# A graph network on one core: which engine subtracts the row maximum of a group's fourth graph

## The chip, the core and the metric

The kernel runs on one core of a Trainium2 chip. The core has five engines with a queue of instructions each: TensorE (PE in the profile; its weight loads stand apart as PEld), VectorE (DVE), ScalarE (ACT), GpSimd (POOL) and SyncE (SP), which here only issues DMAs. Engines wait for each other through semaphores. On-chip memory is SBUF, and PSUM for what TensorE writes. The metric is the device time of one execution in microseconds (us), the median of several runs; lower is better.

## What is computed

64 graphs of 128 nodes with 128 features go through four layers, each on the layer norm and ReLU of what came before and each added to its input: graph attention, a two-layer network on summed neighbours, a graph convolution, and five steps of a gated recurrent unit. The change lies in the softmax of the attention:

```python
def _L0_gnn_ref(x, adj, W, a):
    h = jnp.einsum('bni,io->bno', x, W).reshape(x.shape[0], x.shape[1], H, D)   # H = 4, D = 32
    ...
    e = e_i[:, :, :, None] + e_j[:, :, None, :]
    e = jnp.where(e > 0, e, LRELU_SLOPE * e)
    e = jnp.where(adj[:, None, :, :] > 0, e, NEG_INF)
    attn = jax.nn.softmax(e, axis=-1)
    out = jnp.einsum('bhnm,bhmd->bhnd', attn, h)
    ...
...
h = jnp.maximum(_layernorm(x, axis=-1), 0.0)
x = x + _L0_gnn_ref(h, adj, L0_gnn_W, L0_gnn_a)
h = jnp.maximum(_layernorm(x, axis=-1), 0.0)
x = x + _L1_gnn_ref(h, adj, L1_gnn_eps, L1_gnn_W1, L1_gnn_b1, L1_gnn_W2, L1_gnn_b2)
h = jnp.maximum(_layernorm(x, axis=-1), 0.0)
x = x + _L2_gnn_ref(h, adj, L2_gnn_weight, L2_gnn_bias)
h = jnp.maximum(_layernorm(x, axis=-1), 0.0)
x = x + _L3_gnn_ref(h, adj, nodemask, L3_gnn_weight, L3_gnn_w_ih, L3_gnn_w_hh, L3_gnn_b_ih, L3_gnn_b_hh)
```

## The kernel before

Nodes lie on the 128 partitions, and x stays in SBUF. The graphs are taken in 16 **groups** of four. A first stage (`first_layers`, some 265 us) computes the first three layers, a second one (`gru_layer`) the recurrent layer, with four groups in flight, and it is almost all matmuls.

The first stage is a software pipeline. It has one **slot** a group, and in a slot each engine works on up to eight groups at different depths: `at(n)` is the group that entered n slots ago. The order of each engine's work in a slot is written out by hand in its own `slot(at, number)`; nothing is scheduled or planned. A wait stands in the queue of its engine, and what is behind it waits too.

The attention's scores of a group are made for `at(2)`. TensorE writes the four heads of graph g, with the mask, to PSUM bank g. Then, for g = 0 to 3:

- ScalarE's `leaky` (L1092) takes a leaky ReLU from PSUM to the SBUF tile `prob` (128 x 4 heads x 128), after `score_ready`;
- VectorE's `row_max` (L1259) writes the maximum of each row and head to `row_max` (128 x 4), and raises `max_done`;
- GpSimd's `less_max` (L712) waits for that and subtracts the maximum from `prob` in place, and raises `shifted`;
- ScalarE's `exponential` (L1097) waits for `shifted`; TensorE's `turn_prob` (L862) transposes the heads to PSUM; `keep_probT` copies them back to SBUF, graphs 0 and 2 on ScalarE (L1102), graphs 1 and 3 on VectorE (L1263), graphs 2 and 3 in the next slot.

In the next slot TensorE's `attend` multiplies by the projected nodes, its first half after graphs 0 and 1 and its second after graphs 2 and 3, and `sum_up` takes the softmax's sums. VectorE copies both out (L1267, L1271), takes the reciprocal of the sums when TensorE has transposed them (L891, L1276), multiplies (L1281) and adds to x (L1286). TensorE's last masks of the following group, `mask(at(2), 2)` and `mask(at(2), 3)`, wait for these, since they write the same banks, and its scores stand behind them.

VectorE's slot goes on behind the fourth maximum with `add_out(at(4), 0)` (L1292, x plus the second layer), the `moments` of two layer norms (L1223, L1229), `keep_probT(at(2), 1)` and `add_out(at(5), 1)`. The next slot begins with `shift_of` (L1234), a tiny instruction (128 x 4) that reads `mean_var` and `rstd` in SBUF, for which ScalarE's `normalise` (L1061) waits, and `keep_probT(at(3), 3)`. In slot 4 the largest gate weight is found (`all_rows_max`, L272) just behind the fourth maximum, and TensorE's `turn_max` (L276) waits for it.

GpSimd's slot: `add_self` (L699, adds the self loops to the transposed adjacency), `centre` for layer norm 3 (L721), `bias` (L706), `scale` (L728), `bias`, `scale`, the four `less_max`, and `centre` for layer norm 0, which waits until TensorE has transposed the y of the group before. All are 128 x 512 in SBUF.

Of the kernel before, what the change touches and what calls it, by code (L numbers as in the profile page):

```python
# [24 lines left out]
GRAPHS, NODES, DIM = 64, 128, 128  # L25
HEADS = 4
# [4 lines left out]
GROUP = 4  # L31
# [496 lines left out]
def first_layers(nc, io, t, psum, tiles, gru, score_weights, recurrent, ctx):  # L528

    def sem(name):  # L530
        return ctx.enter_context(nc.semaphore(name))
# [5 lines left out]
    gone, prob, probT, top, attT = tiles.gone, tiles.prob, tiles.probT, tiles.top, tiles.attT  # L537
# [27 lines left out]
    lrelu_done = sem("lrelu_done")  # L565
    max_done = sem("max_done")
    shifted = sem("shifted")
    exp_done = sem("exp_done")
    probT_psum = sem("probT_psum")
    probT_act = sem("probT_act")  # L570
# [121 lines left out]
    def gpsimd(pool):  # L692
        wait_apart = apart(pool, "gpsimd")

        def add_self(group):
            pool.wait_ge(adjT_ready, group.count)
            if group.before(2).exists:
                pool.wait_ge(z_psum[0], group.before(2).count)
            pool.tensor_tensor(adjT1[group.odd][:, :, :], adjT[group.odd][:, :, :],  # L699
                               t["self_eye"][:, :].unsqueeze(1).to_broadcast([128, GROUP, 128]), ALU.add)\  # L700
                .then_inc(adjT1_ready, 1)

        def bias(group, n, b):

            wait_apart(y_ready[n + 1], group.count)
            pool.tensor_tensor(xs(group), xs(group), b[:, :].unsqueeze(1).to_broadcast([128, GROUP, DIM]), ALU.add)\  # L706
                .then_inc(biased[n], 1)

        def less_max(group, g):

            pool.wait_ge(max_done, group.graph_count(g))
            pool.tensor_tensor(prob[:, g, :, :], prob[:, g, :, :],  # L712
                               top[:, g, :].unsqueeze(2).to_broadcast([128, HEADS, NODES]),
                               ALU.subtract).then_inc(shifted, 1)

        def centre(group, n):

            wait_apart(var_ready[n], group.count)
            if group.before(1).exists:
                wait_apart(yT_psum if n == 0 else h0T_psum, group.before(1).count)  # L720
            pool.tensor_tensor(y[n][:, :, :], xs(group), mean_var[n][:, :, 0:1].to_broadcast([128, GROUP, DIM]),  # L721
                               ALU.subtract).then_inc(centred[n], 1)

        def scale(group, n):

            pool.wait_ge(rstd_ready[n], group.count)
            pool.wait_ge(centred[n], group.count)
            pool.tensor_tensor(y[n][:, :, :], y[n][:, :, :],  # L728
                               rstd[n][:, :].unsqueeze(2).to_broadcast([128, GROUP, DIM]), ALU.mult)\
                .then_inc(y_ready[n], 1)  # L730
# [9 lines left out]
        def slot(at, number):  # L740
            if at(4):
                add_self(at(4))
            if at(6):
                centre(at(6), 3)
            if number == 4:
                pool.wait_ge(gru.layers_loaded, gru.all_layers_loaded)
            if at(4):
                bias(at(4), 0, t["b2"])
            if at(6):
                scale(at(6), 3)  # L750
            if at(5):
                bias(at(5), 1, t["b3"])
            if at(1):
                scale(at(1), 0)
            if at(2):
                less_max(at(2), 0)
                less_max(at(2), 1)
                less_max(at(2), 2)
                less_max(at(2), 3)
            if at(0):  # L760
                centre(at(0), 0)

# [282 lines left out]
    def scalar(act):  # L1045
# [47 lines left out]
                .then_inc(lrelu_done, 1)  # L1093

        def exponential(group, g):
            act.wait_ge(shifted, group.graph_count(g))
            a.activation(prob[:, g, :, :], prob[:, g, :, :], ACT.Exp, scale=t["gates_b"][:, E_UNSCALE:E_UNSCALE + 1])\  # L1097
                .then_inc(exp_done, 1)

# [12 lines left out]
        def slot(at, number):  # L1112
# [48 lines left out]
            if at(2):  # L1161
                exponential(at(2), 0)
# [53 lines left out]
    def vector(dve):  # L1216
        v = nc.vector
        wait_apart = apart(dve, "vector")

        def moments(group, n, signal, count):  # L1220
            wait_apart(signal, count)
            for g in range(GROUP):
                last = v.bn_stats(stats[n][:, g, :], t["x"][:, group.graph(g), :])  # L1223
            last.then_inc(stats_done[n], 1)
            wait_apart(stats_done[n], group.count)
            if n in (0, 3) and group.before(1).exists:
                wait_apart(y_ready[n], group.before(1).count)
            for g in range(GROUP):
                last = v.bn_aggr(mean_var[n][:, g, :], stats[n][:, g, :])  # L1229
            last.then_inc(var_ready[n], 1)  # L1230

        def shift_of(group, n):
            dve.wait_ge(rstd_ready[n], group.count)
            v.scalar_tensor_tensor(shift[n][:, :], mean_var[n][:, :, 0], -1.0, rstd[n][:, :], ALU.mult, ALU.mult)\  # L1234
                .then_inc(shift_ready[n], 1)
# [21 lines left out]
        def row_max(group, g):  # L1257
            dve.wait_ge(lrelu_done, group.graph_count(g))
            v.tensor_reduce(top[:, g, :], prob[:, g, :, :], AXIS.X, ALU.max).then_inc(max_done, 1)  # L1259

        def keep_probT(group, g):
            dve.wait_ge(probT_psum, group.graph_count(g))
            v.tensor_copy(probT[:, g, :, :].rearrange("p h n -> p (h n)"), P[:, g, :]).then_inc(probT_dve, 1)  # L1263

        def keep_attended(group):
            dve.wait_ge(att_psum, group.count)
            v.tensor_copy(flat(attT[:, :, :]), P[:, 0, :]).then_inc(att_kept, 1)  # L1267
# [27 lines left out]
        def slot(at, number):  # L1295
            if number == 5:
                gru.whole_max(dve)
            if number == 7:
                gru.max_bits(dve)
            if number == 0:  # L1300
                score_weights.sum_rows(dve)
            if at(4):
                shift_of(at(4), 1)
            if at(3):
                keep_probT(at(3), 3)
            if at(6):
                moments(at(6), 3, x_added[1], at(6).count)
            if number == 18:
                gru.split_hi(dve)
            if at(2):  # L1310
                find_gone(at(2))
            if at(3):
                keep_attended(at(3))
                keep_sums(at(3))
            if at(5):
                shift_of(at(5), 2)
            if at(2):
                keep_e_lo(at(2))
            if at(3):
                divide(at(3))  # L1320
                add_attended(at(3))
            if at(2):
                find_edges(at(2))
            if number == 2:
                score_weights.self_weight(dve)
            if at(3):
                moments(at(3), 1, x_attended, at(3).count)
            if number == 3:
                gru.row_max(dve, 0, 2)
            if number == 18:  # L1330
                recurrent.parts(dve, 0)
            if at(2):
                row_max(at(2), 0)
            if number == 6:
                gru.biases(dve)
            if at(2):
                row_max(at(2), 1)
            if number == 7:
                gru.exponent(dve)
            if at(2):  # L1340
                row_max(at(2), 2)
            if number == 7:
                gru.scale_bits(dve)
            if at(2):
                row_max(at(2), 3)
            if number == 4:
                gru.row_max(dve, 2, 4)
                gru.row_max(dve, 4, 6)
                gru.all_rows_max(dve)
            if at(4):  # L1350
                add_out(at(4), 0, B_TURN)
            if number == 7:
                gru.scales(dve)
            if at(0):
                moments(at(0), 0, x_loaded[at(0).odd], at(0).loads)
            if number == 0:
                score_weights.row_max(dve)
            if number == 1:
                score_weights.whole_max(dve)
                score_weights.scale(dve)  # L1360
            if at(4):
                moments(at(4), 2, x_added[0], at(4).count)
            if number == 7:
                gru.scaled_biases(dve)
            if number == 18:
                gru.split_lo(dve, GRU_STEPS, GRU_STEPS + 1)
            if at(2):
                keep_probT(at(2), 1)
            if at(5):
                add_out(at(5), 1, B_EDGE)  # L1370
# [378 lines left out]
```

## Time and profile before

| | us |
|---|---|
| median of 3 runs | 652.4 (651.42 to 653.29) |
| the profiled execution | 651.48 |
| its span, from first to last instruction | 649.3 |
| TensorE, VectorE, ScalarE, GpSimd busy | 609.8, 574.0, 520.2, 402.8 |

The profile is one execution. Busy shares are taken over both stages. A row of the timeline is: start, length, engine, line, operation, output<-inputs, partitions x elements and type, xN for N alike in a row and, in brackets, the idle time of the engine before it and what ended it. Instructions of one engine overlap a little at their ends. Of line numbers, those of `kernel.py` before the change are meant.

### The profile page before, as it was taken

To read this page: it belongs to the slowest core of one execution; us is meant where nothing else is said; L and a number is where in the kernel's file an instruction comes from. 1 tells how busy PE (TensorE), PEld (TensorE's weight loads), DVE (VectorE), ACT (ScalarE), POOL (GpSimd) and SP (SyncE) were. 2 spreads that over 40 slices of the span, in tenths; PEclk is the share of its full clock that TensorE was granted. 3 is DMA by queue.
4 is the path that set the end of the run, shared out by engine and by line. 5 is a ranking of instruction groups with operands and counts; after the bars stand their busy time and mean duration, and the time that the engine had idled before them with its cause. 6 is when DMAs were issued, how large, how long until landed. Compare 5 with 4: busy or idle time off the path is not lost. (4 is left out here: it accounts for less than half of the span.)

```text
span 649.3 us, 14511 instructions
## 1 busy us (share of the span) xinstructions
PE 609.8 (94%) x5068; PEld 391.4 (60%) x5068; DVE 574.0 (88%) x1384; ACT 520.2 (80%) x964; POOL 402.8 (62%) x363
## 2 busy tenths in 40 slices
PE   2877999999999999799999999999999999999995
PEld 1566887878888888555544455555455555555552
DVE  3478988888998888878898999999999999999995
ACT  2566998999999999667877887877877877877874
POOL 3354677778888776745766655655655655555554
PEclk9888999999999999999999999999999999999998
DMA  7201010101010000112232333433333433333432
GB/s 152 66 18 49 19 49 19 49 19 50 19 51 28 24 18 3 34 36 48 58 57 49 66 64 67 82 78 70 65 63 69 82 82 66 66 81 68 82 80 67
DMA packets 114696, 35.91 MB, mean 55 GB/s; under 512 B 87680, under 2 KB 114624, under 8 KB 114624
## 3 DMA queue, kind: packets, MB, share of 16 engines
q1 hardware_dynamic: 113424, 34.79, 25.2%
q8 instruction: 41, 0.67, 0.4%
q10 hardware_dynamic: 1200, 0.20, 0.2%
q14 instruction: 31, 0.25, 0.1%
HBM read 9.80 MB, written 4.19 MB: 22 GB/s over the span
## 5 line engine op out<-in xcount | busy, mean ns | idle before, releaser
L1650 POOL TENSOR_TENSOR h0T<-r,zh 128x512 f32<-128x512 f32 x80 | 101.6, 1270 | 142.6 <-DVE r L1687 142.3
L52 PE MATMUL psum<-h_parts,gru_w 128*128 128x512 f16 x720 | 183.0, 380 | 2.9 <-DVE r L1691 2.8
L52 PE MATMUL psum<-t_parts,gru_w 128*128 128x512 f16 x720 | 181.5, 379 | 0.0
L52 PEld LDWEIGHTS psum<-h_parts,gru_w 128*128 128x128 f16 x720 | 69.9, 98 | 85.6 <-DVE r L1691 16.1
L1644 POOL TENSOR_TENSOR zh<-z,h0T 128x512 f32<-128x512 f32 x80 | 101.8, 1273 | 11.2 <-ACT z L1622 11.2
L52 PEld LDWEIGHTS psum<-t_parts,gru_w 128*128 128x128 f16 x720 | 66.8, 98 | 66.4 <-DVE t_parts L1674 6.9
L1619 ACT CAST t_parts<-psum 128x512 f16<-128x512 f32 x80 | 46.9, 586 | 62.2 <-PE psum L52 62.1
L1532 DVE CAST h_parts<-h0T 128x512 f16<-128x512 f32 x80 | 79.9, 999 | 3.0 <-POOL h0T L1650 3.0
L1627 ACT ACTIVATE r<-r,gates_b 128x512 f32<-128x512 f32 x80 | 65.0, 812 | 9.5 <-DVE r L1678 6.7
L712 POOL TENSOR_TENSOR prob<-prob,row_max 128x512 f32<-128x512 f32 x64 | 64.5, 1040 | 12.2 <-DVE row_max L1259 11.6
L1622 ACT ACTIVATE z<-psum,gates_b 128x512 f32<-128x512 f32 x80 | 62.3, 778 | 5.8 <-PE psum L52 0.9
L721 POOL TENSOR_TENSOR y<-x_all,mean_var 128x512 f32<-128x512 f32 x32 | 34.4, 1074 | 49.0 <-DVE mean_var L1229 23.7
L1632 ACT ACTIVATE r<-psum,gates_b 128x512 f32<-128x512 f32 x80 | 61.1, 763 | 3.3 <-PE psum L52 3.3
L1691 DVE SCALAR_TENSOR_TENSOR r<-psum,gates_b,r 128x512 f32<-128x512 f32 x80 | 59.6, 744 | 2.3 <-ACT r L1632 2.3
L1624 ACT ACTIVATE zc<-psum,gates_b 128x512 f32<-128x512 f32 x80 | 61.6, 769 | 0.0
L1674 DVE TENSOR_TENSOR t_parts<-psum,t_parts 128x512 f16<-128x512 f32 x80 | 54.6, 682 | 6.2 <-ACT t_parts L1619 6.2
L1687 DVE TENSOR_TENSOR r<-r,zc 128x512 f32<-128x512 f32 x80 | 56.4, 705 | 2.7 <-ACT r L1627 2.7
L1223 DVE BATCH_NORM_STATS2 stats<-x_all 128x6 f32<-128x128 f32 x256 | 54.9, 277 | 4.0 <-DMA x_all<-in_x 3.2
L1534 DVE TENSOR_TENSOR h_parts<-h0T,h_parts 128x512 f16<-128x512 f32 x80 | 55.4, 692 | 2.7
L1061 ACT ACTIVATE y<-x_all,shift,rstd 128x128 f32<-128x128 f32 x128 | 52.7, 488 | 2.5 <-DVE shift L1234 2.4
L1678 DVE TENSOR_TENSOR r<-psum,r 128x512 f32<-128x512 f32 x80 | 54.4, 680 | 0.0
L52 PEld LDWEIGHTS psum<-edges,h_nodes 128*128 128x128 f16 x640 | 42.4, 98 | 18.7 <-issue 0.3
(145 smaller groups left out, 1123.8 us busy)
## 6 DMA issues: line engine op xcount, KB each, us to landing
x_all<-in_x SPq DMA_DIRECT2D x16, 256.0 KB, 4.0
adj<-in_adj SPq DMA_DIRECT2D x16, 256.0 KB, 3.0
out_x<-y SPq DMA_DIRECT2D x14, 256.0 KB, 2.5
h_nodes<-h_parts SPq DMA_TRANSPOSE x80, 3.1
out_x<-zT SPq DMA_DIRECT2D x2, 256.0 KB, 2.3
gw<-in_L_gnn_weight SPq DMA_DIRECT2D x1, 320.0 KB, 5.7
W<-in_L_gnn_W SPq DMA_DIRECT2D x2, 128.0 KB, 2.7
wi<-in_L_gnn_w_ih SPq DMA_DIRECT2D x1, 192.0 KB, 7.1
```

The source lines that it names most:

```text
L52: return nc.tensor.matmul(out, lhsT, rhs, start=start, stop=stop)
L712: pool.tensor_tensor(prob[:, g, :, :], prob[:, g, :, :], top[:, g, :].unsqueeze(2).to_broadcast([128, HEADS, NODES]), ALU.subtract).then_i ...
L1532: v.tensor_copy(by_graph(hp[now.s][:, 0, :]), state(now)).then_inc(hi_ready, 1)
L1534: v.tensor_tensor(by_graph(hp[now.s][:, 1, :]), state(now), by_graph(hp[now.s][:, 0, :]), ALU.subtract)\
L1622: a.activation(z[one.s][:, :], one.Z, ACT.Sigmoid, bias=col(B_Z), scale=col(UNSCALE))\
L1624: a.activation(zc[one.s][:, :], one.Z, ACT.Sigmoid, bias=col(B_NZ), scale=col(N_UNSCALE))\
L1627: a.activation(r[one.s][:, :], r[one.s][:, :], ACT.Tanh, bias=col(B_IN), scale=col(UNSCALE))\
L1632: a.activation(r[here.s][:, :], here.R, ACT.Sigmoid, bias=col(B_R), scale=col(UNSCALE))\
L1644: pool.tensor_tensor(by_graph(zh[now.s][:, :]), by_graph(z[now.s][:, :]), state(now), ALU.mult)\
L1650: pool.tensor_tensor(state(now), by_graph(r[now.s][:, :]), by_graph(zh[now.s][:, :]), ALU.add)\
L1687: v.tensor_tensor(r[two.s][:, :], r[two.s][:, :], zc[two.s][:, :], ALU.mult).then_inc(mixed, 1)
L1691: v.scalar_tensor_tensor(r[one.s][:, :], one.N, col(B_HN), r[one.s][:, :], ALU.add, ALU.mult)\
```

## The change

GpSimd's slot has three `less_max` instead of four. VectorE gets `less_last`, the same subtraction for g = 3, right behind its fourth `row_max`; it waits for that maximum and raises a new semaphore, `last_shifted`. ScalarE's exponential of g = 3 waits for the new semaphore, and those of g = 0 to 2 count three a group.

```diff
@@ -756,7 +757,6 @@
                 less_max(at(2), 0)
                 less_max(at(2), 1)
                 less_max(at(2), 2)
-                less_max(at(2), 3)
             if at(0):
                 centre(at(0), 0)
 
@@ -1093,7 +1093,10 @@
         def exponential(group, g):
-            act.wait_ge(shifted, group.graph_count(g))
+            if g == GROUP - 1:
+                act.wait_ge(last_shifted, group.count)
+            else:
+                act.wait_ge(shifted, group.number * (GROUP - 1) + g + 1)
             a.activation(prob[:, g, :, :], prob[:, g, :, :], ACT.Exp, scale=t["gates_b"][:, E_UNSCALE:E_UNSCALE + 1])\
                 .then_inc(exp_done, 1)
@@ -1258,6 +1261,14 @@
+        def less_last(group):
+
+            g = GROUP - 1
+            dve.wait_ge(max_done, group.graph_count(g))
+            v.tensor_tensor(prob[:, g, :, :], prob[:, g, :, :],
+                            top[:, g, :].unsqueeze(2).to_broadcast([128, HEADS, NODES]),
+                            ALU.subtract).then_inc(last_shifted, 1)
+
@@ -1343,6 +1354,7 @@
             if at(2):
                 row_max(at(2), 3)
+                less_last(at(2))
```

VectorE's queue from the row maxima of a group in the middle of the first stage to the copy of the fourth transposed graph, before:

```order
L1259 TENSOR_REDUCE row_max<-prob 128x4 x4
L1292 TENSOR_TENSOR x_all<-psum,x_all 128x512
L1223 BN_STATS stats<-x_all 128x6 x4
L1229 BN_AGGR mean_var<-stats 128x2 x4
L1223 BN_STATS stats<-x_all 128x6 x4
L1229 BN_AGGR mean_var<-stats 128x2 x4
L1263 COPY probT<-psum 128x512
L1292 TENSOR_TENSOR x_all<-psum,x_all 128x512
L1234 SCALAR_TENSOR_TENSOR shift<-mean_var,rstd 128x4
L1263 COPY probT<-psum 128x512
```

The same with the change (its lines have moved by 3 to 11):

```order
L1262 TENSOR_REDUCE row_max<-prob 128x4 x4
L1268 TENSOR_TENSOR prob<-prob,row_max 128x512
L1303 TENSOR_TENSOR x_all<-psum,x_all 128x512
L1226 BN_STATS stats<-x_all 128x6 x4
L1232 BN_AGGR mean_var<-stats 128x2 x4
L1226 BN_STATS stats<-x_all 128x6 x4
L1232 BN_AGGR mean_var<-stats 128x2 x4
L1274 COPY probT<-psum 128x512
L1303 TENSOR_TENSOR x_all<-psum,x_all 128x512
L1237 SCALAR_TENSOR_TENSOR shift<-mean_var,rstd 128x4
L1274 COPY probT<-psum 128x512
```

One instruction stands between the maxima and the sum that was next; what follows keeps its order.

GpSimd's queue at the same place, from the subtractions to the bias of the next slot, before:

```order
L712 TENSOR_TENSOR prob<-prob,row_max 128x512 x4
L721 TENSOR_TENSOR y<-x_all,mean_var 128x512
L699 TENSOR_TENSOR adjT<-adjT,self_eye 128x512
L721 TENSOR_TENSOR y<-x_all,mean_var 128x512
L706 TENSOR_TENSOR x_all<-x_all,b 128x512
```

With the change:

```order
L713 TENSOR_TENSOR prob<-prob,row_max 128x512 x3
L722 TENSOR_TENSOR y<-x_all,mean_var 128x512
L700 TENSOR_TENSOR adjT<-adjT,self_eye 128x512
L722 TENSOR_TENSOR y<-x_all,mean_var 128x512
L707 TENSOR_TENSOR x_all<-x_all,b 128x512
```

The fourth subtraction is gone, and nothing else has moved.

## Rows read from the trace of the kernel before

**Rows 1.** The page: busy us and share; a group: xcount | busy, mean ns.

```profile
PE 609.8 (94%) x5068; PEld 391.4 (60%) x5068; DVE 574.0 (88%) x1384; ACT 520.2 (80%) x964; POOL 402.8 (62%) x363
...
L712 POOL TENSOR_TENSOR prob<-prob,row_max 128x512 f32<-128x512 f32 x64 | 64.5, 1040 | 12.2 <-DVE row_max L1259 11.6
```

**Rows 2.** Windows: stretch, length, busy of PE PEld DVE ACT POOL, PEclk, DMA.

```profile
36.51:52.71 16.20, 13.36 (x148) 10.30 (x148) 11.22 (x35) 12.07 (x26) 8.63 (x8) 0.89 0.07 18
...
100.64:117.38 16.74, 15.21 (x183) 12.38 (x183) 14.44 (x59) 14.79 (x38) 11.86 (x12) 1.00 0.06 17
117.38:132.06 14.68, 14.68 (x182) 12.31 (x182) 13.10 (x52) 14.55 (x36) 11.86 (x12) 1.00 0.19 55
...
161.43:176.36 14.93, 14.89 (x182) 12.28 (x182) 13.38 (x52) 14.68 (x37) 11.86 (x12) 1.00 0.07 20
...
220.55:235.24 14.69, 14.69 (x182) 12.31 (x182) 13.10 (x52) 14.56 (x36) 11.73 (x12) 1.00 0.07 21
```

**Rows 3.** Timeline of ScalarE in the interval from 146.75: exponentials 2 and 3, normalising.

```profile
151.88 1.34 ACT L1097 ACTIVATE prob<-prob,gates_b 128x512 f32<-128x512 f32 x2
...
154.60 1.66 ACT L1061 ACTIVATE y<-x_all,shift,rstd 128x128 f32<-128x128 f32 x4
```

**Rows 4.** Timeline of VectorE in the same interval.

```profile
147.38 2.46 DVE L1259 TENSOR_REDUCE row_max<-prob 128x4 f32<-128x512 f32 x4 [0.40 <-ACT prob L1092]
149.76 0.68 DVE L1292 TENSOR_TENSOR x_all<-psum,x_all 128x512 f32<-128x512 f32 x1
...
154.23 0.15 DVE L1234 SCALAR_TENSOR_TENSOR shift<-mean_var,rstd 128x4 f32<-128x4 f32 x1
154.30 0.68 DVE L1263 COPY probT<-psum 128x512 f32<-128x512 f32 x1
...
158.31 0.26 DVE L1276 RECIPROCAL rsum<-psum 128x16 f32<-128x16 f32 x1 [0.32 <-PE psum L891]
...
159.34 0.69 DVE L1286 TENSOR_TENSOR x_all<-psum,x_all 128x512 f32<-128x512 f32 x1
```

**Rows 5.** Timeline of TensorE in the same interval: attention's second half, last masks.

```profile
155.15 0.62 PE L52 MATMUL psum<-probT,hW 128*32 128x128 f32 x16
...
160.26 0.59 PE L52 MATMUL psum<-gone,identb 128*128 128x512 bf16 x2
```

**Rows 6.** Timeline of GpSimd in the same interval: subtractions, self loops.

```profile
148.14 4.04 POOL L712 TENSOR_TENSOR prob<-prob,row_max 128x512 f32<-128x512 f32 x4
...
154.31 1.29 POOL L699 TENSOR_TENSOR adjT<-adjT,self_eye 128x512 f32<-128x512 f32 x1
```

**Rows 7.** L1687's durations (ns min/median/max); timelines of VectorE and GpSimd at 315.

```profile
L1687 DVE TENSOR_TENSOR r<-r,zc x80: 681/684/1532, 283.9 to 642.4; 128x512 f32<-128x512 f32 x80
...
315.31 1.53 DVE L1687 TENSOR_TENSOR r<-r,zc 128x512 f32<-128x512 f32 x1
...
315.18 1.11 POOL L721 TENSOR_TENSOR y<-x_all,mean_var 128x512 f32<-128x512 f32 x1
316.44 1.30 POOL L728 TENSOR_TENSOR y<-y,rstd 128x512 f32<-128x512 f32 x1
```

**Rows 8.** Timelines of VectorE and of GpSimd, interval from 161.43.

```profile
168.91 0.44 DVE L1234 SCALAR_TENSOR_TENSOR shift<-mean_var,rstd 128x4 f32<-128x4 f32 x1
...
168.28 1.04 POOL L721 TENSOR_TENSOR y<-x_all,mean_var 128x512 f32<-128x512 f32 x1 [1.42 <-PE psum L803]
169.28 1.28 POOL L699 TENSOR_TENSOR adjT<-adjT,self_eye 128x512 f32<-128x512 f32 x1
```

**Rows 9.** Timelines of VectorE and of GpSimd, interval from 100.64.

```profile
108.60 0.91 DVE L1234 SCALAR_TENSOR_TENSOR shift<-mean_var,rstd 128x4 f32<-128x4 f32 x1
...
108.20 1.29 POOL L699 TENSOR_TENSOR adjT<-adjT,self_eye 128x512 f32<-128x512 f32 x1
```

**Rows 10.** Timeline of TensorE, interval from 52.71.

```profile
57.87 0.27 PE L276 MATMUL psum<-ident,top 128*1 128x128 f32 x1 [3.20 <-DVE top L272]
```

**Rows 11.** Timeline of VectorE, interval from 235.24.

```profile
241.22 0.69 DVE L1263 COPY probT<-psum 128x512 f32<-128x512 f32 x1 [0.75 <-PE psum L862]
```

More of the change, by code:

```diff
@@ L567, in first_layers @@
     shifted = sem("shifted")
+    last_shifted = sem("last_shifted")
     exp_done = sem("exp_done")
```

## The prediction

> I call the stretch from the first leaky ReLU of one group (L1092 on ScalarE) to that of the next an **interval**. There are sixteen such starts, at 20.61 to 249.93 us, and the change acts once behind each.
>
> **What bounds the kernel now.** First the page's busy shares: TensorE 94%, VectorE 88%, ScalarE 80%, GpSimd 62% [rows 1]. They mix two stages. Everything touched here runs in the first 265 us; the recurrent stage behind is a row of matmuls that starts when the first stage lets it. So I split the first stage into its intervals [rows 2]. Eight in a row, from 117.38 to 235.24, are nearly alike: six last 14.68 or 14.69, one 14.83, one 14.93, with VectorE busy 13.10 of 14.68, ScalarE 14.55 and GpSimd 11.86. By busy time ScalarE is the bound and VectorE seems to have 1.6 to spare. The timeline says otherwise. In the interval from 146.75, VectorE ends the shift at 154.23 + 0.15 = 154.38 and the copy of the fourth transposed graph at 154.30 + 0.68 = 154.98 [rows 4]. ScalarE begins normalising, which needs that shift, at 154.60 [rows 3], and TensorE begins the second half of the attention, which needs that copy, at 155.15 [rows 5]. At the far end VectorE's residual sum ends at 159.34 + 0.69 = 160.03 [rows 4] and TensorE's last masks, which need it, start at 160.26; they stand just ahead of the scores for which the next leaky ReLU waits [rows 5]. So a second chain runs VectorE, TensorE, VectorE, TensorE, ScalarE and closes in the same 14.68. Between the row maxima and that copy VectorE has no wait for another engine in it.
>
> The interval from 161.43 shows how little slack that chain has. There the shift took 0.44 where it takes 0.15, 0.29 more [rows 8], and the interval lasted 14.93 where 14.68 is usual, 0.25 more [rows 2]. So a delay ahead of that copy goes into the interval but for 0.04.
>
> **Why that shift was long.** It reads two tensors in SBUF. In the same moment GpSimd ran its centring, 168.28 to 169.32; the shift ended at 169.35, 0.03 behind it, although GpSimd's next instruction had been taken up at 169.28 [rows 8]. In the interval from 100.64 the shift started at 108.60, inside GpSimd's self-loop addition of 108.20 to 109.49, took 0.91 and ended at 109.51 [rows 9]. A full tile does the same: the product at 315.31 took 1.53 where the median of its 80 is 0.684, and ended at 316.84, 0.55 behind GpSimd's instruction (315.18 + 1.11 = 316.29); GpSimd's next one, taken up meanwhile, ended at 317.74, 0.90 behind VectorE's [rows 7]. So a VectorE instruction with two SBUF inputs is held until the running GpSimd instruction ends, and then goes first. The Trainium skill, SBUF — State Buffer, section Who interferes with whom, has this rule: a VectorE instruction with two SBUF inputs and a GpSimd instruction that reads SBUF exclude each other for a whole instruction, the first to issue going first; the trace agrees. With it the interval costs what follows; without it, it would cost the first rival's price.
>
> **The change, part by part, in the interval from 146.75.**
>
> Taken away: the fourth of GpSimd's subtractions, which start 1.00 apart and take 1.04 each, 4.04 for four [rows 1, 6]. Who waits for it? The fourth exponential is the second of the pair at 151.88 to 153.22, and starts some 0.6 in, behind the third; the subtraction ended at 152.18 [rows 3, 6]. Next on GpSimd is a centring that waits for TensorE's transposes, which follow the second exponential, so it does not start earlier. I cost this edit at nothing: ScalarE's third exponential hides it.
>
> Added: on VectorE the same subtraction, with both inputs in SBUF (prob and row_max). The four maxima end at 147.38 + 2.46 = 149.84 [rows 4]. It can't read before GpSimd's second subtraction ends, at 148.14 + 1.00 + 1.04 = 150.18 [rows 6]; whatever its wait for its own maximum takes, up to 0.34, vanishes in that. By the product's row it ends 0.55 later, at 150.73. Not held, it would take 0.684. The residual sum behind it began 0.08 ahead of the maxima's end, at 149.76 [rows 4]; now it begins at 150.65, **0.89 later**. Queued behind it are eight statistics with their means, the copy of the second transposed graph, a residual sum, the shift and the copy of the fourth, all 0.89 late.
>
> Moved by that: GpSimd's third subtraction, held in its turn, ends at 150.73 + 0.90 = 151.63 where it ended at 151.18. The third exponential began at 151.88 [rows 3], so 0.25 is still spare. No cost, but thin cover.
>
> Moved too, and this decides: the shift goes from 154.23 to 155.12. Until now it fell just ahead of the self-loop addition, which starts at 154.31 and ends at 154.31 + 1.29 = 155.60 [rows 6]. That addition follows the centring, which follows TensorE and ScalarE, so it stays. The shift now falls inside it and ends 0.02 behind it, at 155.62, **1.24 later** than 154.38 [rows 4, 6, 9]. That holds for any delay from 0.1 to 1.1, so the price of the subtraction hardly matters. Less the 0.04 of slack: **+1.20 an interval**, 15.88. ScalarE waits about 1.1 for the shift, TensorE 1.2 for the copy. The second half of the interval hangs on these and moves as a whole; VectorE's wait of 0.32 for the transposed sums [rows 4] stays, since that work itself waits for VectorE.
>
> **The other intervals.** The two from 70.86 and 85.50 have the same order: +1.20 each. In the one from 100.64 the shift was already held to the end of the addition at 109.49 [rows 9]; 0.7 to 0.89 later it starts at 109.3 to 109.5 and ends about where it did: 0, at most 0.13. In the one from 52.71 TensorE waited 3.20 for VectorE's largest gate weight (L272), which stands behind the fourth maximum [rows 10]: +0.9, or 0.7 if nothing holds it. In the two from 235.24 and 249.93 VectorE waits 0.75 for a transposed graph behind that point [rows 11], which takes up nearly all of 0.89, and the addition comes earlier there: 0, at most 0.1 each. The first two are full of waits for TensorE: 0, give or take 0.3. The recurrent stage follows in program order and moves as a whole: 0.
>
> **Sum.** 0.9 + 2 x 1.20 + 8 x 1.20 = 12.9. The profiled execution took 651.48 (span 649.3); that gives 664.4. It lay 0.9 under the median of the three runs, 652.4, so for a median I say **665.3**.
>
> **Rivals.**
>
> Nothing is held at the shift. If the addition comes a little later, or such a small instruction slips in, an interval pays only the subtraction, 0.72 to 0.89 less 0.04: ten times 0.68 to 0.85 and 0.7 to 0.9 once, 7.5 to 9.4, so 660 to 662. Against it: both held shifts [rows 8, 9].
>
> GpSimd goes first. If its third subtraction gets the inputs ahead of VectorE's, VectorE starts after 151.18 and ends at 151.73: 1.89 late, 1.85 in ten intervals, about 1 in the one from 100.64, 1.9 in the one from 52.71 and 0.9 in each of the last two: 23, so 675. Against it: at 169.28 the waiting VectorE went first [rows 8]. For it: two full tiles contending have no row here.
>
> TensorE's clock. It idles 1.2 more in 15.9. The interval from 36.51 shows a mean granted clock of 0.89; in the one from 100.64, with 15.21 busy of 16.74, it stayed at 1.00 [rows 2], the 2.4 GHz level. New intervals would have 14.68 of 15.88, 92%, against 91% there, so I expect no fall. If it came, a clock of 0.89 would cost up to 0.11 x 15.9 = 1.7 in each of eight: 14 more, 679.
>
> It is hidden (not slower). If the bound were ScalarE's row of work alone, VectorE's waits of 0.40 ahead of the maxima and 0.32 ahead of the reciprocal [rows 4] would take the 0.72, and the time stays 652, 651.7 if the rare waits on the fourth subtraction go. It decides at the shift: it needs the shift's end to move by less than about 0.1. The Trainium skill, GPSIMD Engine Reference, section Key points, calls VectorE structurally about 2x faster at elementwise work; the rows show 1.04 against 0.684, and that speaks for the swap only where GpSimd's end is waited for. Against this rival: the interval from 161.43.
>
> **Chances.** Forecast 0.67, not held at the shift 0.14, GpSimd first 0.08, clock 0.05, hidden 0.06. The forecast's own range is 663 to 668, by the small terms left at nothing. The range of 8 in 10 takes in the first rival and an early share of the others: 659.5 to 671. Of the hidden case I give 0.02 to faster by over 0.3% (about what a measurement here can tell from no change) and 0.04 to within it; slower has 0.94.
>
> **What would show it.** In the new profile: eight intervals of about 15.9; VectorE's subtraction about 0.85 long; GpSimd's third one about 1.5; the shift about 0.5 long and ending with the self-loop addition; ScalarE's normalising waiting about 1.1 for it; granted clock 1.00; the recurrent stage as long as before. Intervals of 15.4 to 15.5 speak for the first rival, of 16.5 for GpSimd first, of 14.7 for the hidden one. Wrong would be, above all, my claim that the self-loop addition stays where it is while VectorE moves.

## The result and the profile after

The kernel with the change took 663.92 us (663.5 to 664.22, 4 runs) against 651.91 for the one before (650.79 to 653.29, 4 runs), a ratio of 1.0188 with a 95% interval of 1.0161 to 1.0215: **12.0 us slower**, where 12.9 and a time of 665.3 had been forecast. The profiled execution took 663.5, with a span of 661.4.

The windows of the kernel after, from one group's first leaky ReLU to the next one's (columns as in [rows 2]: busy PE, PEld, DVE, ACT, POOL, then the granted clock):

```profile
52.38:72.38 20.00, 15.64 (x163) 12.84 (x163) 16.05 (x49) 13.34 (x31) 7.97 (x7) 0.83 0.15 41
...
104.59:121.32 16.73, 15.44 (x183) 12.40 (x183) 14.29 (x60) 14.78 (x37) 11.32 (x11) 1.00 0.06 17
...
137.20:153.07 15.87, 15.16 (x182) 12.27 (x182) 14.29 (x53) 14.67 (x36) 11.29 (x11) 1.00 0.07 19
153.07:169.16 16.09, 15.38 (x182) 12.35 (x182) 14.41 (x53) 14.71 (x36) 11.51 (x11) 1.00 0.17 50
...
232.65:248.52 15.87, 15.17 (x182) 12.27 (x182) 14.28 (x53) 14.68 (x37) 11.29 (x11) 1.00 0.07 19
248.52:263.20 14.68, 14.68 (x182) 12.30 (x182) 12.92 (x45) 14.29 (x34) 10.69 (x10) 1.00 0.07 20
```

Against [rows 2]: the eight alike intervals have gone from 14.68 to 15.87, one of them to 16.09 (there VectorE's means have a gap of 0.21 that no wait explains); the one that held 16.74 still has 16.73; the last but one is 14.68 as before. The one from 52.38 has grown by 1.85, from the 18.15 between 52.71 and 70.86 in before, more than any.

VectorE's timeline in the interval from 137.20, which answers to [rows 4]:

```profile
140.33 0.85 DVE L1268 TENSOR_TENSOR prob<-prob,row_max 128x512 f32<-128x512 f32 x1
141.10 0.68 DVE L1303 TENSOR_TENSOR x_all<-psum,x_all 128x512 f32<-128x512 f32 x1
...
144.97 0.68 DVE L1303 TENSOR_TENSOR x_all<-psum,x_all 128x512 f32<-128x512 f32 x1
145.57 0.49 DVE L1237 SCALAR_TENSOR_TENSOR shift<-mean_var,rstd 128x4 f32<-128x4 f32 x1
145.98 0.68 DVE L1274 COPY probT<-psum 128x512 f32<-128x512 f32 x1
```

The source row of the new subtraction (durations in ns, min/median/max):

```profile
L1268 DVE TENSOR_TENSOR prob<-prob,row_max x16: 695/851/853, 23.7 to 266.3; 128x512 f32<-128x512 f32 x16
```

GpSimd's, which answers to [rows 6], and ScalarE's, which answers to [rows 3]:

```profile
138.59 3.48 POOL L713 TENSOR_TENSOR prob<-prob,row_max 128x512 f32<-128x512 f32 x3
143.76 1.04 POOL L722 TENSOR_TENSOR y<-x_all,mean_var 128x512 f32<-128x512 f32 x1 [1.69 <-PE psum L803]
144.76 1.28 POOL L700 TENSOR_TENSOR adjT<-adjT,self_eye 128x512 f32<-128x512 f32 x1
...
142.33 1.34 ACT L1100 ACTIVATE prob<-prob,gates_b 128x512 f32<-128x512 f32 x2
...
146.18 1.26 ACT L1061 ACTIVATE y<-x_all,shift,rstd 128x128 f32<-128x128 f32 x3 [1.00 <-DVE shift L1237]
```

The subtraction takes 0.85, and 0.695 at the least. GpSimd's three take 3.48, where three at 1.00 apart would take 3.04: its third one is 0.44 longer. The shift starts at 145.57, inside the self-loop addition of 144.76 to 146.04, and ends at 146.06. The residual sum just ahead of it runs inside the same addition and takes its usual 0.68: one of its two inputs is in PSUM. ScalarE, which had no wait ahead of its normalising [rows 3], waits 1.00 for the shift. The third exponential begins at 142.33, 5.13 into the interval, as before: what GpSimd's third subtraction lost stayed under cover.

### The profile page after: what moved, and what is told of

Same layout as the page of the kernel before. It is cut to its first block and busy times, and to the rows that moved or that the text cites. A ratio compares the mean times of both kernels' runs of the same rounds, so it can differ in the third digit from the quotient of the medians.

```text
span 661.4 us, 14511 instructions
## 1 busy us (share of the span) xinstructions
PE 613.2 (93%) x5068; PEld 391.0 (59%) x5068; DVE 589.5 (89%) x1400; ACT 521.1 (79%) x964; POOL 393.8 (60%) x347
## 5 line engine op out<-in xcount | busy, mean ns | idle before, releaser
L713 POOL TENSOR_TENSOR prob<-prob,row_max 128x512 f32<-128x512 f32 x48 | 55.8, 1189 | 11.9 <-DVE row_max L1262 11.3
```

The lines of the kernel that those rows point to most:

```text
L713: pool.tensor_tensor(prob[:, g, :, :], prob[:, g, :, :], top[:, g, :].unsqueeze(2).to_broadcast([128, HEADS, NODES]), ALU.subtract).then_i ...
```

## Experiments

Each run is compared with the kernel before on the same chip in the same batch, since the median of before went from 649.94 to 651.91 over the batches: after lay 12.0 above before in its own. The edits of the first six runs are made to the kernel after, those of the last section to the kernel before; `...` in a diff stands for lines left out.

### Nobody subtracts the fourth maximum

```diff
                 row_max(at(2), 3)
-                less_last(at(2))
...
-                act.wait_ge(last_shifted, group.count)
+                act.wait_ge(max_done, group.graph_count(g))
```

> The kernel after without VectorE's subtraction: the fourth graph's maximum is not subtracted at all, GpSimd subtracts three, and the fourth exponential waits for the fourth maximum. Theory (GpSimd's fourth subtraction cost nothing, VectorE's is the whole loss): intervals of 14.68 and the time of before, 651.9 within 0.7. Rival (GpSimd's fourth was on a path too, and the change gave part of its loss back): 1 to 3 us under before.

Measured: 650.91 against 650.26, a ratio of 1.0011 (0.9989 to 1.0034). All intervals from 73 us on are those of before to 0.01, but for the one of 14.93 there, which is 14.69 here:

```profile
134.51:149.19 14.68, 14.68 (x182) 12.30 (x182) 13.10 (x52) 14.55 (x37) 10.87 (x11) 1.00 0.07 21
```

GpSimd is busy 10.87 instead of 11.86 and nobody notices. Its fourth subtraction cost nothing, so taking it away could give nothing back, and the loss is all VectorE's. (The profiled execution, 654.19, was the longest of the ten; its first three intervals took 52.3 us where those of before took 50.3, with TensorE longer at its lower clock.)

### The self-loop addition moved ahead of the centring

```diff
         def slot(at, number):
-            if at(4):
-                add_self(at(4))
...
+            if at(3) and number != LAST + 3:
+                add_self(at(3))
             if at(0):
                 centre(at(0), 0)
```

> The kernel after, with GpSimd's self-loop addition moved from the head of a slot to the end of the slot before, behind the three subtractions, where GpSimd waits for TensorE. Theory (the shift is held by that addition): VectorE's shift starts 8.4 us into an interval as before and takes 0.15 instead of 0.50, the copy behind it starts 0.34 earlier, ten intervals of 15.87 become 15.53, and the time falls by 3.4, to 660.5. Rival (the interval pays only VectorE's new subtraction and nothing is held at the shift): intervals stay 15.87, the time 663.9.

Measured: 659.5 against 650.26, 1.0152 (1.0122 to 1.0181): 9.2 above before, where after was 12.0 above. Windows, VectorE and GpSimd of this run:

```profile
135.02:150.56 15.54, 15.17 (x182) 12.28 (x182) 13.96 (x53) 14.68 (x37) 11.32 (x11) 1.00 0.06 18
...
143.39 0.15 DVE L1237 SCALAR_TENSOR_TENSOR shift<-mean_var,rstd 128x4 f32<-128x4 f32 x1
143.46 0.68 DVE L1274 COPY probT<-psum 128x512 f32<-128x512 f32 x1
...
139.86 1.28 POOL L700 TENSOR_TENSOR adjT<-adjT,self_eye 128x512 f32<-128x512 f32 x1
141.58 1.04 POOL L722 TENSOR_TENSOR y<-x_all,mean_var 128x512 f32<-128x512 f32 x1 [0.44 <-PE psum L803]
```

The shift starts 8.37 into its interval, as in after, but now GpSimd has nothing running there, and it takes 0.15. Intervals are 15.53, to the hundredth that was forecast. So 0.34 of the 1.19 was the hold at the shift. No instruction of VectorE was touched. The time is less clear than the intervals: the span is 2.8 under after's, not 3.4. The intervals are together 4.7 shorter, 1.2 of it in the one from 52.76, where TensorE's clock was low for less long, and the recurrent stage is 1.7 longer, with a low stretch that after lacks (both below).

### One head instead of four

```diff
-            v.tensor_tensor(prob[:, g, :, :], prob[:, g, :, :],
-                            top[:, g, :].unsqueeze(2).to_broadcast([128, HEADS, NODES]),
+            v.tensor_tensor(prob[:, g, 0:1, :], prob[:, g, 0:1, :],
+                            top[:, g, 0:1].unsqueeze(2).to_broadcast([128, 1, NODES]),
                             ALU.subtract).then_inc(last_shifted, 1)
```

> The kernel after, with VectorE's subtraction cut to one of four heads (128 x 128 instead of 128 x 512); for the fourth graph the other three heads' maxima are not subtracted. Theory: the subtraction ends some 0.4 earlier, the shift starts at 7.97 instead of 8.37 us of an interval, is still inside the self-loop addition and ends with it, so the intervals stay 15.87 and the time stays 663.9 within 0.5. Rival (the price goes with the subtraction's length): intervals of 15.5, 4 us less, 659.9.

Measured: 663.51 against 650.26, 1.0213 (1.0186 to 1.0239), within 0.5 of after's 663.92, as forecast (13.3 above its own before, with the intervals of after). The subtraction's source row, the window, VectorE's shift and GpSimd's addition:

```profile
L1268 DVE TENSOR_TENSOR prob<-prob,row_max x16: 291/452/455, 23.9 to 266.2; 128x128 f32<-128x128 f32 x16
...
137.02:152.90 15.88, 14.94 (x182) 12.25 (x182) 14.30 (x53) 14.68 (x36) 10.91 (x11) 1.00 0.06 18
...
145.00 0.89 DVE L1237 SCALAR_TENSOR_TENSOR shift<-mean_var,rstd 128x4 f32<-128x4 f32 x1
...
144.59 1.28 POOL L700 TENSOR_TENSOR adjT<-adjT,self_eye 128x512 f32<-128x512 f32 x1
```

VectorE does 0.40 less in each interval and the interval is as long as ever. The shift comes 0.40 earlier and takes 0.40 longer, 0.89, until the addition ends at 145.87. By the busy share VectorE is as full as in after (14.30 of 15.88 against 14.29 of 15.87): the hold counts as busy.

### Both edits

> Both edits of the two runs before it: one head on VectorE (three heads' maxima of the fourth graph not subtracted) and the self-loop addition ahead of the centring. Theory: now the subtraction's length counts, since nothing holds the shift: it ends at about 8.12 us of an interval, intervals of 15.13, time 656.5. Rival: the same as with one head alone.

Measured: 656.6 against 650.26, 1.0101 (1.0073 to 1.0129).

```profile
133.88:149.02 15.14, 14.94 (x182) 12.25 (x182) 13.56 (x53) 14.67 (x36) 10.91 (x11) 1.00 0.07 20
...
141.85 0.15 DVE L1237 SCALAR_TENSOR_TENSOR shift<-mean_var,rstd 128x4 f32<-128x4 f32 x1
```

Now the 0.40 counts in full: 15.53 less 0.40 is 15.13. The four runs make a square of interval lengths:

| | addition behind the centring | addition ahead of it |
|---|---|---|
| four heads on VectorE | 15.87 | 15.53 |
| one head | 15.88 | 15.13 |

The subtraction's length has no effect in one column and its whole effect in the other. No price put on the subtraction alone can give that; a hold that ends with a GpSimd instruction does.

### The shift moved to another place

VectorE's queue alone is changed: both sets of statistics ahead of both sets of means, the shift between the means of the slot before, the residual sum ahead of the second copy.

```diff
-            if at(4):
-                shift_of(at(4), 1)
...
+            both = at(0) and at(4)
+            if both:
+                stats_of(at(0), 0, x_loaded[at(0).odd], at(0).loads)
+                stats_of(at(4), 2, x_added[0], at(4).count)
+                means_of(at(0), 0)
+                shift_of(at(3), 1)
+                means_of(at(4), 2)
```

> The kernel after, with VectorE's queue changed: both sets of statistics stand ahead of both sets of means (which saves the two waits of 0.26 and 0.15 for its own results), the shift of the second layer norm stands between the means, one slot earlier than its place ahead of the fourth copy, and the residual sum ahead of the copy of the second transposed graph. Theory (the shift's place among GpSimd's instructions made the difference between 0.85 and 1.20): the shift starts near 6.4 us of an interval, just ahead of GpSimd's centring at 6.56, is held by nothing, and the copy of the fourth graph starts at 8.04: intervals of 15.13, time 656.6 by the clock of the run after (8 to 9 us under it is too much, 7 is right). Rival (a hold always costs the same, wherever the shift stands): only the 0.4 of waits goes, intervals of 15.47.

Measured: 654.6 against 649.94, 1.0073 (1.0052 to 1.0094), 7.3 less above before than after was. The edit moves the residual sum, which the diff does not show. Window, the subtraction, the shift and the two copies behind it:

```profile
133.64:148.63 14.99, 14.76 (x182) 12.34 (x182) 13.76 (x53) 14.55 (x37) 11.30 (x11) 1.00 0.07 19
...
136.76 0.85 DVE L1274 TENSOR_TENSOR prob<-prob,row_max 128x512 f32<-128x512 f32 x1
...
139.96 0.14 DVE L1243 SCALAR_TENSOR_TENSOR shift<-mean_var,rstd 128x4 f32<-128x4 f32 x1
...
140.87 1.29 DVE L1280 COPY probT<-psum 128x512 f32<-128x512 f32 x2
```

The shift is not held, ScalarE does not wait for it, and the second copy of the pair starts at 7.82 of the interval, not 8.04: the reordering saved 0.2 more than I had counted. The interval follows: 7.82 is 0.27 later than before's 7.55, and 14.99 is 0.31 longer than 14.68, where 15.13 had been forecast. So three quarters of the loss can be had back while VectorE still does the subtraction; how much of them is the hold and how much the two waits saved, this run alone does not tell.

### The largest gate weight first

```diff
                 row_max(at(2), 3)
-                less_last(at(2))
             if number == 4:
                 gru.row_max(dve, 2, 4)
                 gru.row_max(dve, 4, 6)
                 gru.all_rows_max(dve)
+            if at(2):
+                less_last(at(2))
```

> The kernel after, with VectorE's new subtraction moved, in the fourth slot alone, behind the search for the largest gate weight. The interval from 52.4 grew from 18.14 to 20.00, where 0.9 had been forecast. Theory (0.7 of it is the subtraction ahead of that search, 1.2 is TensorE at its lower clock level for 6.8 us there instead of 3.4): TensorE waits 3.2 for the weight instead of 4.08, and the interval is 18.1 with one low stretch of 3.4, 19.3 with one of 6.8. Rival (the whole 1.9 is the subtraction): 18.1 either way.

One run: 664.06; no verdict on the time is possible from it. The interval came to 18.11 with one low stretch of the clock, which both theories gave. What tells them apart is the same interval in the other runs. After and the self-loops run both had the subtraction ahead of the search, and TensorE waited equally long for the weight, 4.08 and 4.09; but after had the lower clock level for 6.8 us, the self-loops run for 3.4. The wait of after, a window around its low stretch, the low stretch of the self-loops run, and then the interval in that run and in this one:

```profile
58.42 0.37 PE L276 MATMUL psum<-ident,top 128*1 128x128 f32 x1 [4.08 <-DVE top L272]
...
57.40:64.30 6.90, 5.88 (x27) 5.58 (x28) 4.67 (x22) 3.01 (x6) 0.00 (x0) 0.51 0.40 113
...
58.50:61.90 3.40, 3.10 (x14) 2.80 (x15) 3.00 (x18) 1.84 (x4) 1.18 (x1) 0.50 0.15 43
52.76:71.58 18.82, 14.35 (x163) 11.49 (x163) 15.82 (x49) 13.36 (x32) 8.00 (x7) 0.91 0.15 44
...
53.14:71.25 18.11, 14.53 (x163) 11.67 (x163) 16.02 (x49) 13.35 (x32) 7.53 (x7) 0.91 0.16 45
```

With a mean granted clock of 0.91 the interval is 18.11 with the subtraction behind the search and 18.82 with it ahead: 0.7 is its price. With a mean of 0.83 it is 20.00 in after: 1.2 more, which goes with TensorE at 1.2 GHz for 6.8 us instead of 3.4. The place of the self-loop addition makes no difference there: with one head the interval is 19.65 with the addition behind the centring and 19.69 with it ahead, both with 6.8 us of the lower level. Why the level stayed down twice as long is not shown, and the length of the wait does not tell: 4.09 went with 3.4 in the self-loops run and with 6.8 in the run with the shift moved. In before, which waited 3.20 until 57.87, the stretch began at 58.5, behind the wait; in after it began at 57.4, inside the wait. The recurrent stage of this run had a low stretch, 399.84 against after's 398.20, which takes back most of what the interval gained.

### Is there room in the kernel before?

The same three edits of VectorE's queue, made to the kernel before:

> The kernel before with the same three edits of VectorE's queue, and no subtraction on it. Theory (in before two chains tie at 14.68, VectorE's and ScalarE's row of work): VectorE's copy can start 0.26 earlier, but ScalarE is full, so intervals stay 14.68 and the time stays that of before within 0.7. Rival (VectorE's chain alone sets the interval): intervals of 14.42, 2.6 to 3.4 less.

> The kernel before with VectorE's queue changed, a second time and in more rounds. Intervals of 14.68 as in the first; it lay 0.25% under before, which is the two stray delays of 0.25 and 0.15 in the profile of before and the clock in the recurrent stage. Theory: 0.1 to 0.4% under before. Rival: no difference.

Measured: 649.27 against 649.94, 0.9975 (0.9953 to 0.9997), and again 649.69 against 650.16, 0.998 (0.9961 to 0.9998). The intervals from 117 us on are 14.68, all of them: VectorE's copy comes earlier (7.29 into the interval for 7.55) and the interval is no shorter, as it must if another row of work is full. What has changed is the intervals that were longer in before:

```profile
101.53:117.14 15.61, 14.96 (x183) 12.45 (x183) 13.50 (x59) 14.66 (x38) 11.87 (x12) 1.00 0.07 18
```

That is the interval of 16.74 in [rows 2], whose shift took 0.91 [rows 9]: 1.1 shorter, of which 0.76 is the length of the hold; the rest fits the waits that the new order saves, and the two were not separated. The one of 14.93, whose shift was held too, is at 14.68, and so is the one of 14.83, whose shift had taken 0.15: there VectorE's means had a gap of 0.17 that no wait explains. Together that is 1.5, of which the time shows some 0.5 to 0.7; in both profiles of this version TensorE's clock was low for longer in the first three intervals, which came to 52.1 instead of 50.3, and not low at all at the start of the recurrent stage (below). So a gain is shown in the intervals, most of it from the moved shift; how much of the 0.2% is it and how much the clock is not.

Then, with VectorE's queue as in the last run, ScalarE was relieved too, and the self-loop addition put behind the subtractions:

```diff
+        def root_0(group):
+            pool.tensor_tensor(log_var[0][:, :], mean_var[0][:, :, 1], eps_tile[:, :], ALU.add)\
+                .then_inc(eps_added[0], 1)
+            pool.wait_ge(eps_added[0], group.number - 1)
+            pool.tensor_tensor(rstd[0][:, :], log_var[0][:, :], half_tile[:, :], ALU.pow).then_inc(rstd_ready[0], 1)
...
-            if at(1):
+            if at(1) and number < 3:
                 rstd_of(at(1), 0)
```

> The run before it (before with VectorE's queue changed) with ScalarE relieved as well: from the third group on, the inverse deviation of the first layer norm (two ScalarE instructions, 0.48 a slot) is computed by GpSimd behind its centring, with the power that it uses for the last groups, and the self-loop addition stands behind the subtractions. Theory (both chains shorter): ScalarE's row needs 14.20, VectorE's copy of the fourth graph can't start before TensorE's transposes end, at 7.29 instead of 7.55 of an interval, so intervals of about 14.42, and 2.5 to 3.5 less than before. Rival (ScalarE alone sets the interval): 14.20, 5 less.

Measured: 652.26 against 649.94, 1.0034 (1.0011 to 1.0058), with intervals of 15.22. I had walked into the thing under study. The shift had been moved to 5.43 of the interval and the self-loop addition, by the other edit, to the same moment:

```profile
139.37 1.25 DVE L1249 SCALAR_TENSOR_TENSOR shift<-mean_var,rstd 128x4 f32<-128x4 f32 x1
...
139.32 1.28 POOL L699 TENSOR_TENSOR adjT<-adjT,self_eye 128x512 f32<-128x512 f32 x1
```

So the addition was made to wait for the shift:

```diff
         def add_self(group):
             pool.wait_ge(adjT_ready, group.count)
+            pool.wait_ge(shift_ready[1], group.count)
```

> The run with both chains relieved again, but GpSimd's self-loop addition waits until the shift is made. In that run the moved shift, at 5.43 us of an interval, had met the addition, which had been moved to the same place: it took 1.25 instead of 0.14, and the intervals came to 15.22. Theory: with the wait the shift takes 0.14, VectorE's copy of the fourth graph starts when TensorE's transposes end (7.3), ScalarE's row is 0.48 shorter, and the intervals are 14.4, the time 2.5 to 3.5 under before. Rival (something else was late there, TensorE's own row or the extra GpSimd work): intervals of 14.7 or more.

Measured: 649.04 against 650.16, 0.9982 (0.9965 to 1.0). The hold is gone, the interval still is not shorter, and the rival was right:

```profile
131.54:146.23 14.69, 14.69 (x182) 12.32 (x182) 13.00 (x52) 14.30 (x34) 13.19 (x14) 1.00 0.06 19
...
136.98 0.13 DVE L1250 SCALAR_TENSOR_TENSOR shift<-mean_var,rstd 128x4 f32<-128x4 f32 x1
...
146.23 1.08 ACT L1102 ACTIVATE prob<-psum 128x512 f32<-128x512 f32 x2 [0.28 <-PE psum L52]
...
PEld psum L52 <- DVE x_all L1302: 1.7, 5, 0.3
```

With both of the others relieved, ScalarE waits 0.28 for TensorE's scores at the head of the interval. The last line is from the waits of five intervals: TensorE's weight loads wait 0.3 in each for VectorE's residual sum, and no wait listed there is for GpSimd, so its extra work does not show as the bound. A third row of work, TensorE's with that short wait in it, closes in 14.68 too. That it is the bound is read from these waits and was not tested by taking one of its instructions away. This version and the one with VectorE's queue alone are the fastest of those run, some 0.2% under before, by a margin hardly clear of none.

## Why the prediction was right

Taken step by step:

- **The two chains that tie at 14.68**: right. The chain through VectorE turned a delay of 1.23 into 1.19 in the seven undisturbed of the eight alike intervals, as the one stray interval [rows 2, 8] had said. There is a third tie, TensorE's row. The prediction took ScalarE for the bound by busy time, though [rows 2] has TensorE busy 14.68 of 14.68; it changes nothing for a delay.
- **GpSimd's fourth subtraction at nothing**: right, shown by the run in which nobody does it.
- **VectorE's subtraction, 0.89**: right. It took 0.85 where GpSimd was subtracting and 0.695 at the least; the sum behind it begins 3.90 into the interval, as forecast, against 3.01.
- **GpSimd's third, 0.45 later, under cover**: right; 3.48 for three, and the third exponential did not move.
- **The shift held to the end of the self-loop addition**: right, and shown by the square of four runs. It ended 8.86 into the interval, 1.23 later. ScalarE's wait was 1.00 and not 1.1.
- **The other intervals**: 1.23 and 1.20 for the two from 70.86 and 85.50, nothing for the one from 100.64, nothing for the one from 235.24: right. The one from 100.64, already held, shows that a hold does not add up with a delay: its shift took 0.91 in before and 0.17 in after.
- **The interval from 52.71**: a term mis-sized. 0.9 was put down, or 0.7 if nothing holds the subtraction; it measured 1.85, of which 0.7 is the subtraction ahead of the search and 1.2 goes with TensorE's clock.
- **The recurrent stage, 0**: off by 1.2 the other way. From the last group's leaky ReLU to the end it went from 399.37 to 398.20:

```profile
268.00:285.00 17.00, 13.16 (x66) 7.40 (x67) 13.72 (x31) 9.57 (x16) 9.29 (x9) 0.90 0.23 45
...
264.00:290.00 26.00, 21.44 (x209) 17.31 (x208) 22.87 (x70) 19.18 (x42) 17.42 (x15) 1.00 0.11 22
```

The first row is before, the second after, both at the start of the recurrent stage. Before has a stretch of TensorE at the lower level there, after has none. Over the twelve profiles of this case, the seven with such a stretch took 399.4 to 400.1 from the last group's leaky ReLU to the end and the five others, among them both of the version with VectorE's queue changed, 397.6 to 398.2.

The intervals together grew by 13.4 (229.32 to 242.73), against 12.9 forecast; the recurrent stage gave 1.2 back, and the start 0.1: 12.1 in the span, 12.0 in the medians. TensorE's clock went with 1.2 us more in the interval from 52.71 and with some 1.2 less in the recurrent stage; that the two cancel is luck. The ten intervals of the mechanism itself came to 11.8 where 12.0 had been forecast. The rival on the clock was priced for the eight alike intervals, where nothing of it came, and not for the places where the clock was low already.

## What to carry to other kernels

In this kernel a VectorE instruction with two inputs in SBUF, even one of 128 x 4, could not be priced by its own length where GpSimd worked beside it: find the GpSimd instruction that will be running when it is issued, and take that one's end. So a delay on VectorE can cost more than itself, or nothing, by where it moves such an instruction; before moving work between these two engines, lay their two timelines over each other for every two-input instruction behind the edit. And an engine with 38% of its time free, as GpSimd here, may be worth nothing to relieve; a run in which the moved work is done by nobody tells that.

## What was not expected of the hardware

The prediction said that two full tiles contending had no row. [rows 7] is one: the product at 315.31 went ahead of the GpSimd instruction taken up at 316.44, and that is the same order as here. Where both waited, VectorE's instruction went first: the new full-tile subtraction was issued during GpSimd's second one, 0.26 ahead of GpSimd's third being taken up, and the third took 1.5 instead of 1.04. The opposite order of arrival, with both waiting, was not looked into.

What was not expected is where a hold shows. The length of a small instruction is the best gauge of it: the shift took from 0.12 to 1.27 us in these runs, all of it counted as VectorE's busy time: in after and in the run with one head VectorE is equally busy, with 0.40 of work between them. A busy share does not tell held from working.
